# Cross-attention on one core: the row of maxima issued from ScalarE's queue, keys and queries stacked earlier, weight cutting reordered on GpSimd

## The reference, cut to what matters

```python
qh = q.reshape(B, S, KV, G, D).transpose(0, 2, 3, 1, 4)      # B=4, S=512, KV=8, G=4, D=16
kh = k.reshape(B, S, KV, D).transpose(0, 2, 1, 3)            # k = v = ctx_512, (4, 512, 128)
scores = jnp.einsum('bkgsd,bktd->bkgst', qh, kh) / scale
weights = jax.nn.softmax(scores, axis=-1)
out = jnp.einsum('bkgst,bktd->bkgsd', weights, vh)
x = _layernorm(x + out)
```

## Time and profile before

| | us |
|---|---|
| median of 3 runs | 2573.51 (2572.28 to 2574.54) |
| the profiled execution's own time | 2594.45 |
| its span, first to last instruction | 2592.7 |
| cross-attention stage, from its first DMA to the next stage's | 486.96 to 1050.85 |

### The profile page before, as it was taken

The page is one execution under the profiler, slowest core; times in us unless marked ns, Lnnn a source line. Parts: engine busy times, 40 slices in busy tenths (PEclk is TensorE's granted clock), DMA queues, the critical chain, the costliest instruction groups (busy, mean ns, idle before and its releaser), DMA issues. The chain is left out here.

```text
span 2592.7 us, 33108 instructions
## 1 busy us (share of the span) xinstructions
PE 2025.5 (78%) x12220; PEld 1362.0 (53%) x12252; DVE 1739.4 (67%) x2695; ACT 1247.0 (48%) x2228; POOL 771.5 (30%) x872
## 2 busy tenths in 40 slices
PE   5999999377778787688887499999940479889990
PEld 4777787222222222355554378787830357667760
DVE  3546565376767675789997445556659855379986
ACT  2233232167555556367777423223229541178971
POOL 1111213201594950121110121122315204055525
PEclk8899999678888989899997689999975789889995
DMA  5332322456343420400000332223210030099966
GB/s 154 82 74 50 74 50 50 142 143 175 86 142 88 143 59 7 185 1 1 1 1 1 98 73 65 56 53 74 50 65 1 0 117 1 4 408 423 414 276 194
DMA packets 84591, 264.62 MB, mean 102 GB/s; under 512 B 17504, under 2 KB 19040, under 8 KB 73424
## 3 DMA queue, kind: packets, MB, share of 16 engines
q0 software_dynamic: 29632, 151.50, 17.5%
q1 hardware_dynamic: 53776, 110.75, 15.1%
q10 hardware_dynamic: 1024, 0.26, 0.0%
HBM read 169.87 MB, written 41.72 MB: 82 GB/s over the span
## 5 line engine op out<-in xcount | busy, mean ns | idle before, releaser
L921 DVE TENSOR_REDUCE x_negm<-x_M 128x2 f32<-128x1024 f32 x256 | 309.4, 1224 | 112.8 <-PE x_M L981 112.2
L870 ACT ACTIVATE x_PT<-x_T 128x512 f32<-128x512 f32 x512 | 279.9, 598 | 201.5 <-PE x_T L1001 196.3
L327 ACT ACTIVATE L_attn_PT<-L_attn_T 128x512 f32<-128x512 f32 x320 | 175.5, 595 | 359.0 <-PE L_attn_T L559 359.0
L409 DVE TENSOR_REDUCE L_attn_negm<-L_attn_M 128x2 f32<-128x1024 f32 (+1 forms) x192 | 192.1, 1041 | 57.2 <-PE L_attn_M L540 57.1
L234 POOL DMA_DIRECT2D L_attn_QKS<-L_attn_HL x64 | 34.8, 544 | 599.0 <-ACT L_attn_HL L312 565.1
L1001 PE MATMUL x_T<-x_QS,x_KS 49*128 49x512 f32 x512 | 141.1, 548 | 64.5 <-ACT x_PT L870 44.9
L557 PE MATMUL L_attn_T<-L_attn_QKS 97*128 97x256 f32 (+3 forms) x512 | 166.2, 386 | 8.4 <-DMA L_attn_QKS<-L_attn_mT 6.1
L1001 PEld LDWEIGHTS x_T<-x_QS,x_KS 49*128 49x128 f32 x512 | 52.1, 200 | 214.4 <-ACT x_PT L870 131.2
L1010 PE MATMUL x_O<-x_PT,x_V 128*32 128x512 f32 x1024 | 155.6, 684 | 8.3 <-issue 8.3
L538 PE MATMUL L_attn_M<-L_attn_QKS 96*128 96x384 f32 (+2 forms) x384 | 139.7, 434 | 28.1 <-DVE L_attn_XTL L383 11.5
L981 PE MATMUL x_M<-x_KS,x_QS 48*128 48x512 f32 x512 | 119.1, 463 | 42.1 <-DMA x_QS<-x_xl 23.4
(11 more groups left out here) (394 smaller groups left out, 5568.0 us busy)
## 6 DMA issues: line engine op xcount, KB each, us to landing
L_attn_QKS<-L_attn_HL SPq DMA_DIRECT2D x192, 128.0 KB, 4.7
L_attn_QKS<-L_attn_HL POOLq DMA_DIRECT2D x192, 128.0 KB, 3.9
moe_y_rows<-slots_YS SPq DMA_DIRECT2D x47, 256.0 KB
x_WRAW<-in_w_gateT POOLq DMA_DIRECT2D x8, 1024.0 KB, 7.5
x_QS<-x_xh SPq DMA_DIRECT2D x128, 64.0 KB, 2.4
x_WRAW<-in_w_upT POOLq DMA_DIRECT2D x8, 1024.0 KB, 5.2
x_WRAW<-in_w_downT POOLq DMA_DIRECT2D x8, 1024.0 KB, 6.3
ffn_w<-x_WTER POOLq DMA_DIRECT2D x12, 512.0 KB, 3.7
```

Source lines behind the costliest of these rows:

```text
L327: ac.activation(PT[:, s, bank], T[:, bank], ACT.Exp, scale=SCALE).then_inc(t_free, 1)
L409: last = ve.tensor_reduce(negm[:, g % 2, h0:h0 + nh, i], src, AX.X, ALU.max, negate=True)
L870: ac.activation(PT[:, s // 4, head(s), :], T[(STEPS_S * g + s) % 3][:], ACT.Exp, scale=SCALE).then_inc(t_free, 1)
L921: ve.tensor_reduce(negm[:, g % 2, u // 4:4:2, u % 4], m[:].rearrange("p (r k) -> p r k", r=2), AX.X, ALU.max, negate=True).then_inc(m_free, 1)
```

## The change

`shift_row` leaves SP's queue for ScalarE's, at the place of `mt` in `plan`. Along with it: the context is loaded and split one batch first; the first batch of x is unloaded in two halves, the first queries are stacked by SP before any keys, and both halves of the first keys are stacked from ScalarE's queue; the `xt` units move one group earlier, the unload stands in group 4 and SP no longer waits for it before the keys; TensorE's wait for GpSimd's memsets moves behind the first transposes; the weight fetches begin when the first row has landed, and the 24 pieces begin two later; the first four moment steps come one to a `max` unit, from the fifth; and on GpSimd the cuts now follow each batch's layer norm: chunks 0 and 1, then 2 to 4, then 5 to 11.

```diff
-                if in_batch == 4 and s in (11, 13) and b + 1 < NB:
+                if in_batch == 3 and s in (11, 13) and b + 1 < NB:
...
+        def stack_keys(queue, b, lo, hi):
+            for r in range(2):
+                for n, part in enumerate((0, 1, 0)):
+                    rows = slice(LOW * r + HD * n, LOW * r + HD * (n + 1))
+                    src = CP[part][HD * lo:HD * hi, b, :].rearrange("(j d) s -> d j s", d=HD)
+                    queue.dma_start(KS[rows, lo:hi].bitcast(F32), src).then_inc(keys[lo], 16)
+
         block = ctx.enter_context(nc.Block())
 
         @block.sync
         def _(sp):
-            sp.dma_start(CT[:], A["ctxT"].rearrange("b e s -> e b s")).then_inc(ctx_in, 16)
-            sp.dma_start(CTOK[:].rearrange("p (b i) e -> p b i e", b=NB),
-                         A["ctx_512"].rearrange("b (i p) e -> p b i e", p=P)).then_inc(tok_in, 16)
+            ctxT = A["ctxT"].rearrange("b e s -> e b s")
+            sp.dma_start(CT[:, 0:1, :], ctxT[:, 0:1, :]).then_inc(ctx_in, 16)
 
             def unload_x(b):
                 sp.wait_ge(hi_done, 2 * b + 2)
                 sp.dma_start(XP[b % 2][0], XTH[:].bitcast(F32)).then_inc(x_out, 16)
                 sp.wait_ge(m_free, drained("xt", (b, 1)))
                 sp.dma_start(XP[b % 2][1], XTL[:].bitcast(F32)).then_inc(x_out, 16)
-                sp.wait_ge(x_out, 32 * (b + 1))
+
+            def unload_first_x(half):
+                ks = slice(2 * half, 2 * half + 2)
+                sp.wait_ge(hi_done, half + 1)
+                sp.dma_start(XP[0][0][:, ks, :], XTH[:, ks, :].bitcast(F32)).then_inc(x_out, 16)
+                sp.wait_ge(m_free, drained("xt", (0, half)))
+                sp.dma_start(XP[0][1][:, ks, :], XTL[:, ks, :].bitcast(F32)).then_inc(x_out, 16)
...
-            def shift_row(g):
-                sp.wait_ge(m_free, drained("mt", g))
-                for r in range(2):
-                    row = LOW * r + R
-                    sp.dma_start(QS[row:row + 1, g % 4].bitcast(F32).rearrange("p h (i q) -> p (h i) q", i=NT),
-                                 mT[2 * NT * r:2 * NT * (r + 1), :].bitcast(F32)).then_inc(shifted, 16)
-
-            sp.wait_ge(ctx_hi, 1)
-            sp.dma_start(CP[0], CH[:].bitcast(F32)).then_inc(ctx_out, 16)
-            sp.wait_ge(ctx_lo, 1)
-            sp.dma_start(CP[1], CL[:].bitcast(F32)).then_inc(ctx_out, 16)
-            unload_x(0)
-            sp.wait_ge(ctx_out, 32)
-            sp.wait_ge(ones_set, 4)
-            stack_keys(0, 0, 4)
+            unload_first_x(0)
+            sp.wait_ge(x_out, 32)
             stack_queries(0)
             stack_queries(1)
-            stack_keys(0, 4, 8)
+            ctx_tokens = A["ctx_512"].rearrange("b (i p) e -> p b i e", p=P)
+            sp.dma_start(CTOK[:, 0:NT, :], ctx_tokens[:, 0]).then_inc(tok_in, 16)
+            sp.dma_start(CT[:, 1:NB, :], ctxT[:, 1:NB, :]).then_inc(rest_in, 16)
             stack_queries(2)
-            shift_row(0)
+            sp.dma_start(CTOK[:, NT:, :].rearrange("p (b i) e -> p b i e", b=NB - 1), ctx_tokens[:, 1:]).then_inc(more_in, 16)
+            unload_first_x(1)
             for g in range(GROUPS):
                 b, j = g // KV, g % KV
                 if g >= 1:
                     sp.wait_ge(t_full, STEPS_S * g)
+                if g == 1:
+                    sp.wait_ge(x_out, 64)
+                if g == 3:
+                    sp.wait_ge(ctx_hi, 2)
+                    sp.dma_start(CP[0][:, 1:NB, :], CH[:, 1:NB, :].bitcast(F32)).then_inc(ctx_out, 16)
+                    sp.wait_ge(ctx_lo, NB)
+                    sp.dma_start(CP[1][:, 1:NB, :], CL[:, 1:NB, :].bitcast(F32)).then_inc(ctx_out, 16)
                 if j == 5 and b + 1 < NB:
-                    unload_x(b + 1)
-                    stack_keys(b + 1, 0, 4)
+                    sp.wait_ge(x_out, 32 * (b + 3))
+                    if b == 0:
+                        sp.wait_ge(ctx_out, 64)
+                    stack_keys(sp, b + 1, 0, 4)
                 if g + 3 < GROUPS:
                     stack_queries(g + 3)
+                if j == 4 and b + 1 < NB:
+                    unload_x(b + 1)
                 if j == 0 and b >= 1:
-                    stack_keys(b, 4, 8)
-                if g + 1 < GROUPS:
-                    shift_row(g + 1)
+                    stack_keys(sp, b, 4, 8)
...
+                pool.wait_ge(shifted, 32)
...
-            for b in range(NB - 1):
-                cut_weights((range(0, 2), range(2, 7), range(7, 12))[b])
+            for b, chunks in enumerate((range(0, 2), range(2, 5), range(5, 12))):
                 pool.wait_ge(m_free, drained("turn", KV * b + KV - 1))
                 gp.tensor_tensor(Z[b % 2][:], Z[b % 2][:], X[:, b, :, :], ALU.add).then_inc(added, 1)
                 pool.wait_ge(moments, MOMENTS * (b + 1))
                 for i in range(NT):
                     gp.tensor_scalar(X[:, b, i, :], Z[b % 2][:, i, :], ln["mean"][:, i:i + 1], ln["rstd"][:, i:i + 1],
                                      ALU.subtract, ALU.mult).then_inc(applied, 1)
+                cut_weights(chunks)
...
+            def shift_row(g):
+                act.wait_ge(m_free, drained("mt", g))
+                for r in range(2):
+                    row = LOW * r + R
+                    act.dma_start(QS[row:row + 1, g % 4].bitcast(F32).rearrange("p h (i q) -> p (h i) q", i=NT),
+                                 mT[2 * NT * r:2 * NT * (r + 1), :].bitcast(F32)).then_inc(shifted, 16)
+
+            sizes = [(n // 4, 4 * (n % 4) + 2) for n in range(2, 26)]
...
+                    if x[2] == (0, 1):
+                        act.wait_ge(ctx_hi, 1)
+                        act.dma_start(CP[0][:, 0:1, :], CH[:, 0:1, :].bitcast(F32)).then_inc(ctx_out, 16)
+                        act.wait_ge(ctx_lo, 1)
+                        act.dma_start(CP[1][:, 0:1, :], CL[:, 0:1, :].bitcast(F32)).then_inc(ctx_out, 16)
+                        act.wait_ge(ones_set, 4)
+                        act.wait_ge(ctx_out, 32)
+                        stack_keys(act, 0, 0, 4)
+                        stack_keys(act, 0, 4, 8)
+                elif x[0] == "M" and x[1] == "mt":
+                    shift_row(x[2])
                 elif x[0] == "S":
                     g, s = x[1:]
+                    if g == 0 and s == 4:
+                        make_values(0)
+                    if g == 0 and s == 0:
+                        act.wait_ge(rest_in, 16)
+                        ac.activation(CH[:, 1:NB, :], CT[:, 1:NB, :], ACT.Copy).then_inc(ctx_hi, 1)
...
-                    if g < 6 and s % 4 == 2:
-                        piece = 4 * g + s // 4
+                    if (g, s) in sizes:
+                        piece = sizes.index((g, s))
...
                     delay -= 1
                     if delay < 0:
                         next(pending, None)
+                    if delay < -NT:
                         next(pending, None)
                 elif kind == "mt":
                     if arg >= 1:
                         dve.wait_ge(shifted, 32 * arg)
                     ve.tensor_copy(mT[:, :], m[0:4 * NT, 0:P]).then_inc(m_free, 1)
+                    if 1 <= arg < NB:
+                        dve.wait_ge(ctx_hi, 2)
+                        split_context(slice(arg, arg + 1))
...
-                        delay, pending = 5, layernorm_moments(b)
+                        delay, pending = 4, layernorm_moments(b)
...
-            t.wait_ge(ones_set, 4)
...
+                        if arg == (0, 0):
+                            t.wait_ge(ones_set, 4)
```

More of the change, by code:

```diff
@@ L648, in stage_cross_attention @@
         CP = [dram(part, (P, NB, S)) for part in ("ch", "cl")]
-        ctx_in, tok_in, ones_set = sem("ctx_in"), sem("tok_in"), sem("ones_set")
+        more_in = sem("more_in")
+        ctx_in, rest_in, tok_in, ones_set = sem("ctx_in"), sem("rest_in"), sem("tok_in"), sem("ones_set")
         ctx_hi, ctx_lo, ctx_out = sem("ctx_hi"), sem("ctx_lo"), sem("ctx_out")
@@ L721, in stack_queries @@
                         sp.dma_start(QS[rows, g % 4].bitcast(F32), src).then_inc(stacked[g % 4], 16)
-            def stack_keys(b, lo, hi):
-                for r in range(2):
-                    for n, part in enumerate((0, 1, 0)):
-                        rows = slice(LOW * r + HD * n, LOW * r + HD * (n + 1))
-                        src = CP[part][HD * lo:HD * hi, b, :].rearrange("(j d) s -> d j s", d=HD)
-                        sp.dma_start(KS[rows, lo:hi].bitcast(F32), src).then_inc(keys[lo], 16)
-            def shift_row(g):
-                sp.wait_ge(m_free, drained("mt", g))
-                for r in range(2):
-                    row = LOW * r + R
-                    sp.dma_start(QS[row:row + 1, g % 4].bitcast(F32).rearrange("p h (i q) -> p (h i) q", i=NT),
-                                 mT[2 * NT * r:2 * NT * (r + 1), :].bitcast(F32)).then_inc(shifted, 16)
-            sp.wait_ge(ctx_hi, 1)
```

(25 more changed lines are left out.)

11 lines of the change are left out of this document (4 added, 7 removed).

## The result

| | before | after |
|---|---|---|
| median of the runs, us | 2574.03 (2572.28 to 2575.83, 4 runs) | 2627.41 (2621.29 to 2635.26, 4 runs) |
| ratio after / before | | 1.020, 95% interval 1.018 to 1.0221 |
| profiled execution, us | 2594.45 (span 2592.7) | 2628.5 (span 2626.7) |
| stage, from its first DMA to the first instruction of the next | 486.96 to 1050.86: 563.9 | 483.34 to 1099.94: 616.6 |

The change costs 53 us, 2.0%. The two profiled executions stand only 34 us apart, but not because of this stage: behind it the one before takes 2592.7 - 1050.9 = 1541.8 us and the one after 2626.7 - 1099.9 = 1526.8, for work that the change does not touch. Each stage length is read from one profiled execution.

The account below looks back on a forecast made before the run. No engine is full, so waits between engines bound the kernel. Up to batch 2's norm -14 - 25 - 10 + 26 = -23, GpSimd's tail +48.6, giving +26: 2573.5 + 26 = 2600 us, range 2582 to 2624.

Parts of the forecast that it names:

- the sum up to the norm: Start, rows, moments and ScalarE's row: -14 - 25 - 10 + 26 = -23 us, norm of batch 2 starting at 947.1.
- GpSimd's tail: Seven cuts behind batch 2's norm make GpSimd end the stage: +48.6 us, with the shift of -23 a total of +26.
- near 1072: Sign to look for: GpSimd's cut of the last chunk ends near 1072, the next stage following its write.
- VectorE ended 40 us before GpSimd: Sign at the stage's end: VectorE's last step (L990) has ended some 40 us before GpSimd's end.
- The gains up to the norm of batch 2: Terms before that norm: start -14, rows no longer behind keys -25, moments -10 us.
- The start, -14: Stage start: first keys and queries issued 16.1 us earlier, 2 given back for sharing; 14 us gained, bounds 5 and 21.
- Rows no longer behind keys, -25: Changes of batch: the row of maxima no longer queues behind unload and keys in SP's queue; 25 us gained, 11 to 33.
- rows that land as late as before: Rival by the DMA interleaving rule: rows gain at least 11 us instead of 25, total 2614; chance 0.10.
- Moments, -10: Layer norm moments: GpSimd adds at once; 4 us gained for batches 0 and 1 each, 2 for batch 2; bounds 2 and 20.
- The row in ScalarE's queue, +26: Groups: ScalarE's wait and issues delay E10, 0.8 us without pieces, 1.8 with four; 26 us lost before 970.13, bounds 0 and 52.
- My second rival: ScalarE's wait costs its full 2.0 us per group, TensorE's clock falling in the gap: +52, 2626 us; chance 0.07.
- 15.6: Sign to look for: length in us of groups with weight pieces, beside 13.9 for groups without.

Follow-up runs that it names:

- the square: Stages of the change, 9, run 10 and Run 12 compared by row place (before step 10 or behind step 11) and cuts: 616.6, 568.7, 526.9, 574.7 us.
- Run 12: The change with the row alone moved behind the exp of step 11, seven cuts still last: ratio 1.0025 to the kernel before, stage 574.7 us.
- run 10: The change with the row behind the exp of step 11 and cuts ordered 1, 4, 4, 3: 2552.87 us, ratio 0.9861 to the kernel before.
- run 6: The kernel before with GpSimd's twelve cuts spread over its idle times, one between each add and norm: 2589.22 us, ratio 1.0008.
- 11: The kernel before with only GpSimd's cuts reordered, one before the first add, then four, four and three behind the norms: ratio 0.9963.
- Run 2: The change with the old order of cuts and the row back in SP's queue: 2578.29 us, ratio 1.0023 to the kernel before.
- run 5: The kernel before with the row in ScalarE's queue, issued behind the exp of step 11: 2589.43 us, ratio 1.0012.
- run 4: The kernel before with GpSimd's cuts behind the norms, seven behind the last: 2607.35 us, ratio 1.0149.
- 3: The kernel before with only the row moved to ScalarE's queue, at the change's place: 2614.83 us, ratio 1.0153.
- 9: The change with cuts one before the first add, then four, four and three behind the norms, row before step 10: ratio 0.9997 to the kernel before.

## Why the prediction was right or wrong

It forecast 2600 us, slower by 26, in 2582 to 2624; 2627.41 lies 3 us outside and the loss is twice the size. The direction and the engine that ends the stage were right, the sum up to the norm was not. By its steps:

- **GpSimd's tail: right.** 129.4 us from norm to next stage, measured 132.9; the square gives 48 us for it, where the prediction had 48.6. The last cut ended at 1092.2 and not near 1072, by the shift that did not come.
- **VectorE ended 40 us before GpSimd: wrong.** It ends at 1093.05, beside the issue of the last write, because its steps are held up beside the cuts. It cost nothing here, since GpSimd's write ends the stage.
- **The gains up to the norm of batch 2.** The table splits them by where they arise, from the copies of the maxima, as differences from the kernel before in us. Run 12 is the change without the early row's cost, run 10 the same with the cuts 1, 4, 4, 3; the last column has that cost in it.

| stretch | forecast | run 12 | run 10 | the change |
|---|---|---|---|---|
| up to the first copy | -14 | -14.6 | -14.7 | -14.5 |
| the six distances behind it | 0 | +14.0 | +11.2 | +23.2 |
| the three with a change of batch | -25 | -25.5 | -23.0 | -17.0 |
| the six with moments | -10 | -22.0 | -18.8 | -6.7 |
| the rest, up to the norm | 0 | +6.7 | +1.3 | +15.5 |
| sum | -49 | -41.4 | -44.0 | +0.5 |

- **The start, -14: right where it is read, lost behind it.** The first maxima come after 21.8 instead of 36.3 us, 14.5. But S0 waits 4.09 us for the first row at 523.33, and in run 12 the first two distances are 16.9 and 17.9, at granted clocks of 0.50 and 0.64; before they were 13.3 and 13.8, at 0.56 and 1.00. By the seventh copy run 12 is 0.6 us ahead of the kernel before, and run 10 is 3.5. I had carried the 14 to the norm whole. Some 3 us of this come and go by themselves (in runs 6 and 11, where only GpSimd's cuts differ, the second distance is 16.6); the rest has no experiment of its own.
- **Rows no longer behind keys, -25: right in size.** TensorE's waits for the row fell from 19.5 to 5.5 us as forecast, and the row landed sooner: in run 12 it is used at the changes of batch at most 4.9 us after its issue, for 8.8, 8.3 and 7.2 before.

```profile
734.66 1.29 ACTq L855 DMA_DIRECT2D x_QS<-x_mT  x2
...
739.55 0.50 PE L1041 MATMUL x_T<-x_QS,x_KS 49*128 49x512 f32 x2 [0.71 <-DMA x_QS<-x_mT]
```

  The gain is not owed to ScalarE's queue. Run 2 has it with the row in SP's queue (-25.8 in these three distances), and run 5, the queue alone, has -5.4, no more than run 4 (-5.7), whose queues are untouched. What runs 2 and 12 share against the kernel before is the unload moved away from the keys, with the rest of the change around it; no run has that move alone. The rival "rows that land as late as before" (0.10) did not come true in the change; it is true of run 5.
- **Moments, -10: mis-sized.** Run 4, the order of cuts alone, has 26.2 in these distances, and runs 12 and 10 have 22.0 and 18.8. The adds at once save 8 to 10 us in each of three batches in run 4, not 4, 4 and 2.
- The gains came to 41 to 44 us where I had 49. That this is near is luck in part: the start's 14 were lost again, and the moments gave about as much more than forecast.
- **The row in ScalarE's queue, +26: mis-sized, and this is the term that decided.** It costs 42 us in the stages, 35 to 45 by the ratios. The delay of 0.75 us for a group at full clock was right (0.8), and 31 x 0.75 = 23. The rest, 19 us, lies in groups that fell to a lower granted clock: 16 distances over 16 us, where run 12 has 8. I had allowed 1.8 us for a group with pieces and nothing for the clock; they last 17.4 and not 15.6. My second rival had this mechanism and nearly this time (2626, with 52 for the row where 42 is measured) and I gave it 0.07, because stretches as loose as the earlier trace rows ran at 1.00. The same looseness in another place did not.
- The gap between forecast and result, 27 us, is then 16 from the row (42 for 26), 8 from the gains (41 for 49, by run 12) and 3.5 from the tail, mostly because the next stage begins 7.5 us after the issue of the last write and not 4.9.

What stays open: why the clock falls with this gap and not with the gap of the same ScalarE time two exps later. The runs show that it does, three times over (3 against 5, 9 against 10, the change against 12), and not what in the row's place does it: the missing product, the longer wait of S12 or the drift of VectorE's work. The wait for the copy and the 1.3 us of issue were moved together, and were not priced one by one. Open as well is what slows the first groups after the earlier start.

## What to carry to other kernels

An issue in a compute engine's queue costs by its place: the same DMAs cost 42 us of stage ahead of the exp that frees the next product's buffer, and nothing to be measured two exps later, where that engine waits in any case. Look for such a hole before you choose the queue. Do not carry a gain at a stage's start to its end unread: here 14 us were ahead at the first group and 1 to 4 at the seventh, in runs 12 and 10. When several terms of a sum are bounds from distant rows, give the rival that takes the upper end of the costliest one more than a few per cent; and when work is taken off one engine's head and put at its tail, ask for a third place: in run 10 GpSimd's cuts stand behind the earlier norms, and the norm of batch 2 comes no later than in run 12.

## What the hardware showed that I had not expected

VectorE's small SBUF steps can stand still while GpSimd works on SBUF. In the kernel after, beside the last cuts, L77 takes 3.64 us and L74 3.90 where the same steps take 0.15 and 0.16; L74 ends at 1076.07, GpSimd's subtraction at 1076.04. The four last subtractions of VectorE take 16.35 us together, across a whole cut, and 2.29 in run 10 with GpSimd idle. In the same stage the reductions from PSUM keep their 1224 ns: 59 of them run beside a cut, and the longest takes 1230. The three lines of after, with run 6's above, show it in groups of the page's kind (busy us, mean ns):

```profile
L954 DVE TENSOR_REDUCE x_negm<-x_M 128x2 f32<-128x1024 f32 x236 | 286.2, 1224 | 105.8 <-PE x_M L1019 105.2
...
L990 DVE TENSOR_SCALAR X<-x_Z,x_x_ln_mean,x_x_ln_rstd 128x512 f32<-128x512 f32 x4 | 16.2, 4061 | 0.1
...
L77 DVE TENSOR_TENSOR x_x_ln_rstd<-x_x_ln_rstd,x_x_ln_tmp 128x4 f32<-128x4 f32 x16 | 9.8, 612 | 0.1
```

The Trainium skill has the rule for it (SBUF — State Buffer, "Who interferes with whom"): VectorE and GpSimd share one pair of ports, held as an exclusive lock for a whole instruction; VectorE contends for it with steps in a two-port mode, and with steps of two SBUF inputs when GpSimd's reads SBUF. These rows agree for the subtraction. Beside a comparison they show something else:

```profile
1066.47 5.44 POOL L824 TENSOR_SCALAR x_WTER<-x_WRAW,x_cut 128x2048 bf16<-128x2048 f32 x1
1070.24 0.16 DVE L74 TENSOR_TENSOR x_x_ln_tmp<-x_x_ln_rstd 128x4 f32<-128x4 f32 x1
1070.64 1.30 DVE L76 TENSOR_SCALAR x_x_ln_tmp<-x_x_ln_tmp 128x4 f32<-128x4 f32 x1
```

L77 is let through at 1070.20 and L74 runs behind it in 0.16 us, while the comparison lasts until 1071.91; so for steps of two inputs the hold ended 1.7 us before GpSimd's instruction did. The next TENSOR_SCALAR, L76, was held to its end.
